# A transformer of top-1 and top-4 expert layers: the landing waits inside GpSimd's runs of indirect transfers, taken out of the top-4 layers

## The reference, cut to what matters

```python
x = x + 0.5 * top1(norm(x))       # 8 experts, hidden 512, one expert per token
x = x + attention_a(norm(x))      # 8 heads of 128
x = x + 0.5 * top1(norm(x))
x = x + 0.5 * top4(norm(x))       # 32 experts, hidden 128, four per token, and a shared expert of 512
x = x + attention_b(norm(x))      # 16 heads of 8, rotated
x = x + 0.5 * top4(norm(x))

def top4(x):
    scores = softmax(x @ router_w.T + bias)
    w, idx = top_k(scores, 4); w = w / clip(w.sum(), 1e-12)
    h = silu(x @ gate[e].T) * (x @ up[e].T)            # for each of the token's four experts e
    out = sum over the four of w[e] * (h @ down[e].T)
    return out + (silu(x @ sgate.T) * (x @ sup.T)) @ sdown.T
```

## Time and profile before

| | |
|---|---|
| median of 3 runs | 1868.67 us (1867.82 to 1871.08) |
| the profiled execution's own time | 1873.8 us |
| its span, first to last instruction | 1872.0 us |
| PE busy | 1221.8 us (65%) |
| DVE busy | 1135.0 us (61%) |
| POOL busy | 968.9 us (52%) |
| ACT busy | 785.3 us (42%) |
| first top-4 layer, first scatter to the next layer's start | 640.6 to about 1034 us of the span |
| second top-4 layer, first scatter to the end | 1473.5 to 1872 us |

### The profile page before, as it was taken

One profiled execution on the slowest core, in us unless ns is written; L12 is line 12 of the kernel. 1 busy time (PEld: TensorE's weight loads), 2 busy tenths in 40 slices (PEclk: granted clock), 3 DMA queues, 4 the chain that ended last, 5 costly groups with the idle time before them and its releaser, 6 DMA issues.

```text
span 1872.0 us, 34469 instructions
## 1 busy us (share of the span) xinstructions
PE 1221.8 (65%) x11513; PEld 902.4 (48%) x11545; DVE 1135.0 (61%) x2883; ACT 785.3 (42%) x1164; POOL 968.9 (52%) x1052
## 2 busy tenths in 40 slices
PE   2298577874594165979654578777874085979661
PEld 2297455653494024968522244444433035969420
DVE  6546756767357951424467699898987942325442
ACT  2153356661252022534311388887883022535210
POOL 0624234551623276636675377666651376646664
PEclk9998789995796577989967555555555587989886
DMA  9233134410231013645311000000000014536312
GB/s 348 65 96 95 36 123 149 147 54 2 93 90 43 13 49 109 197 132 185 124 48 42 13 2 2 2 1 2 1 2 1 23 48 139 188 131 192 96 49 78
DMA packets 100000, 150.44 MB, mean 80 GB/s; under 512 B 21409, under 2 KB 54817, under 8 KB 99105
## 3 DMA queue, kind: packets, MB, share of 16 engines
q1 hardware_dynamic: 58656, 75.30, 12.3%
q0 software_dynamic: 20480, 41.98, 7.5%
q10 hardware_dynamic: 20736, 31.47, 5.2%
HBM read 74.16 MB, written 74.45 MB: 79 GB/s over the span
## 4 chain that ended last, share of the span: by engine, by line
PE 33%; POOL 19%; DVE 18%; issue 14%; DMA 8%; SPq 4%; ACT 2%; DVEq 0%; ACTq 0%; another core or an unknown queue 0%; POOLq 0%
POOL slots_top L624 14%; POOL AREA L1086 5%; PE PS L845 4%; PE PS L906 4%; DMA slots_top<-XN,ROW 3%; PE PS L298 3%; SPq L1285 3%; DVE X L1107 3%; PE PS L300 3%; PE PS L299 3%; PE PS L1729 2%; PE PS L928 2%; DVE AREA L1895 2%; PE PS L1745 2%; PE PS L1717 2%
## 5 line engine op out<-in xcount | busy, mean ns | idle before, releaser
L624 POOL DMA_INDIRECT slots_top<-XN,ROW x320 | 317.3, 992 | 322.8 <-DVE ROW L578 183.6
L1086 POOL DMA_INDIRECT AREA<-results_top,ROW x320 | 305.2, 954 | 275.2 <-DMA results_top<-AREA 125.1
L998 DVE SCALAR_TENSOR_TENSOR AREA<-PS,AREA 128x512 f32<-128x512 f32 x96 | 66.4, 691 | 254.2 <-ACT AREA L975 251.6
L1690 POOL TENSOR_TENSOR AREA<-AREA 128x1024 f16<-128x1024 f32 x64 | 151.4, 2365 | 91.5 <-ACT AREA L1830 91.3
L906 PE MATMUL PS<-WGU,AREA 128*128 x768 | 187.0, 388 | 0.0
L1919 DVE TENSOR_REDUCE AREA<-PS 128x4 f32<-128x1024 f32 x128 | 156.1, 1219 | 30.4 <-PE PS L1717 29.6
L1823 ACT ACTIVATE AREA<-PS,AREA 128x1024 f32<-128x1024 f32 x128 | 142.6, 1114 | 53.1 <-PE PS L1729 52.9
L906 PEld LDWEIGHTS PS<-WGU,AREA 128*128 128x128 f32 x768 | 142.3, 195 | 16.5 <-ACT AREA L965 0.2
L1318 POOL TENSOR_TENSOR AREA<-AREA 128x1536 f16<-128x1536 f32 x32 | 92.9, 2902 | 102.7 <-ACT AREA L1533 102.7
L417 PE MATMUL PS<-IDF,XN 128*128 128x128 f32 x192 | 49.7, 417 | 134.6 <-DVE XN L407 134.6
L1830 ACT ACTIVATE AREA<-AREA 128x1024 f16<-128x1024 f32 x128 | 135.5, 1059 | 0.0
(11 more groups left out here) (260 smaller groups left out, 3584.9 us busy)
## 6 DMA issues: line engine op xcount, KB each, us to landing
AREA<-slots_top SPq DMA_DIRECT2D x96, 256.0 KB
results_top<-AREA ACTq DMA_DIRECT2D x96, 256.0 KB
slots_top<-ZERO SPq DMA_DIRECT2D x24, 512.0 KB, 3.1
AREA<-slots_top SPq DMA_DIRECT2D x48, 128.0 KB
results_top<-AREA ACTq DMA_DIRECT2D x48, 128.0 KB
AREA<-query_rows SPq DMA_DIRECT2D x48, 128.0 KB, 2.8
slots_top<-XN,ROW POOLq DMA_INDIRECT x320, 2.2
AREA<-results_top,ROW POOLq DMA_INDIRECT x320
```

Source lines behind the costliest of these rows:

```text
L624: nc.gpsimd.indirect_dma_start(out=L.xs[q], out_offset=bass.IndirectOffsetOnAxis(ap=ROW[:, n:n + 1], axis=0), in_=XN[:, t * D:(t + 1) * D] ...
L1086: nc.gpsimd.indirect_dma_start(out=slots[L.tag][u][:, c * D:(c + 1) * D], out_offset=None, in_=L.ys[g * GT // L.tiles], in_offset=bass.Ind ...
L1690: nc.gpsimd.tensor_tensor(PB1[1][:, g, :], PF1[:, g, :], PB1[0][:, g, :], ALU.subtract).then_inc(b_plo[1].sem, 1)
```

## The change

Two conditions are changed. In the top-4 layers GpSimd no longer waits for a landing within dispatch (12 waits a layer, the last of each part among them) nor within combine (12 waits a layer). The top-1 layers keep every wait that they had. The waits for row numbers, for stored results and for a buffer that was added stay everywhere, and so do the waits of SP and DVE for the landings that they need.

```diff
@@ dispatch_pool
                     in_=XN[:, t * D:(t + 1) * D], in_offset=None).then_inc(dp_sent[q].sem, 16)
-                every = (16, 8)[q] if L is L1 else (0, 4)[q]
+                every = (0, 4)[q] if L is L0 else 0
                 if every and n % every == every - 1:
                     pool.wait_ge(*dp_sent[q].at(16 * (n % (L.tiles * L.K) + 1)))
@@ combine_pool
                     ).then_inc(cb_got[u].sem, 16)
-                    if c % 8 == 7 and (g < NG // 2 or c < GK - 1) or L is L0 and c == 3 and g < NG // 2:
+                    if L is L0 and c == 3 and g < NG // 2:
                         pool.wait_ge(*cb_got[u].at(16 * (L.turn[g] * GK + c + 1)))
```

## The result

The changed kernel takes **1806.78 us** (median of 4 runs, 1800.57 to 1807.19) where the one before takes 1868.66 us (1867.82 to 1871.08) on the same chip: a ratio of 0.9664, 95% interval 0.965 to 0.9677, so 3.4% faster. Forecast were 1805 us. The profiled execution took 1806.83 us, with a span of 1805.0 us against 1872.0 us before.

The account below looks back on a forecast made before the run. GpSimd's dispatch and combine in the two top-4 layers were taken to bound the kernel. 26.6 + 37.5 = 64.1 us, less 0.6 us, gave 1810.3 us profiled and a predicted median of 1805 us, range 1798 to 1833 us.

Parts of the forecast that it names:

- The removed waits cost their idle time: Full gain in both top-4 layers: 26.6 and 37.5 us from subtracted idle times; chance 0.76.
- Part 1, the dispatch: Top-4 dispatch: without its waits, part 1's blocks come 17.5 us and 19.8 us earlier in the two layers.
- PE's readiness: Before part 1's blocks: PE ready 15.6 and 16.8 us earlier, data 16.0 and 17.2 us; the smaller counts.
- The slow start between the parts: PE's first slow matmuls after its pause before part 1 go with the pause: 1.9 and 3.0 us.
- A fall of the clock inside the blocks: Sign of being wrong: PE's granted clock falls in 170 us of pauseless blocks; each 1% at 1.2 GHz costs 1.7 us.
- Part 2: First top-4 layer's combine: DVE's 9.06 us before g3 go as well, so g3's addition is 26.6 us earlier.
- GpSimd's wait for buffers: First top-4 combine: waits for buffers hardly bind; g2 and g3 would start at 862.8 and 882.8 us.
- Part 3: Second top-4 layer's combine: g4 starts 31.3 us earlier, four later waits give 6.2 us; g7's addition 37.5 us earlier.
- The idle time of about 5 us: Second top-4 layer: GpSimd stands about 5 us before g4, put down to DVE's L1107.
- Half of it comes: Rival: back-to-back transfers land late, so dispatch's or combine's gain fails; 1831 or 1842 us, chance 0.11.
- The waits only change their name: Rival: GpSimd's descriptor writing stops anyway, the pause returns inside transfer rows; no gain, 1869 us, chance 0.05.
- slower by GpSimd's descriptor writing: Rival: descriptor writing gets dearer from a run's 17th transfer on, 65 us a layer, about 1998 us; chance 0.08.

Follow-up runs that it names:

- e9: The kernel before, unchanged, run again for its trace: 1869.67 us, ratio 1.0002.
- e11: Against the changed kernel, the landing waits of the top-1 layers removed too: 1805.64 us, ratio 0.9664 to the kernel before.
- e3: Against the changed kernel, the combine's waits of g4 to g7 in the top-4 layers kept: 1813.0 us, ratio 0.9727 to the kernel before.
- e7: Against the changed kernel, top-4 combine groups take buffers in another turn, so g4 waits for no addition: 2279.39 us on the second job's chip.
- e1: Against the kernel before, only the dispatch's waits in the top-4 layers removed: 1831.6 us, ratio 0.982.
- e2: Against the kernel before, only the combine's waits in the top-4 layers removed: 1837.28 us, ratio 0.9862.
- e12: Against the changed kernel, a landing wait after every fourth scatter of the top-4 dispatch: 1902.0 us, ratio 1.0169 to the kernel before.
- control: The changed kernel itself, run on the second job's chip: 2278.34 us, ratio 1.0465 to the kernel before.

## Why the prediction was right, and where it was not

**The removed waits cost their idle time.** Right: 26.6 and 37.5 us forecast, 25.6 and 36.6 us measured; the sum 64.1 against 62.2 us, the median 1805 against 1806.78 us. That single terms fit to 1 us is in part luck: `e9`'s trace in the place of before's would give 28.5 and 33.2 us. The sum, then 61.8 us, isn't luck.

**Part 1, the dispatch.** 17.5 and 19.8 us forecast at the first gather, 16.6 us (199.62 to 183.02 us from the first scatter) and 19.6 us (201.87 to 182.27 us) measured. The data are there 15.95 and 17.1 us earlier, by the last scatter's start (16.0 and 17.2 forecast), and PE's readiness is the smaller count, as forecast: no pause is left between the parts, and 3.9 instead of 3.7 us came off before part 0. The slow start between the parts did go. What is missing in the first layer, 0.9 us, is less than what two executions of the kernel before differ by: in `e9` the first gathers come at 201.3 and 199.3 us. In this execution part 0's first L906 took 3.64 us, against 2.92 us before. After g0's addition L906 is slow once more, at 2.72 us, with a granted clock of 0.83 in the 10 us around it. A fall of the clock inside the blocks was one of the signs of being wrong, and it came, if briefly: g1 and g2 are 14.9 us earlier where g0 is 16.6 us earlier, so it took 1.7 us. It doesn't come from the change, though. PE stands there for 1.9 us in `e9` as well, which has the slow step too (24.7 us from g0's addition to g1's, as in after), and `e11`, without the waits, has none (23.1 us, as in before). PE in order of time, and the window (the last three columns are clock, DMA share and GB/s):

```profile
858.17 1.21 PE L928 MATMUL PS<-WD,AREA 128*128 x8 [1.88 <-DVE AREA L993]
...
860.88 2.72 PE L906 MATMUL PS<-WGU,AREA 128*128 x8
```

```profile
856.00:866.00 10.00, 8.12 (x46) 7.30 (x45) 4.81 (x10) 3.02 (x6) 7.56 (x9) 0.83 0.52 147
```

**Part 2.** Right: the 9.06 us before g3 are gone, g3 comes 24.1 us earlier (26.6 forecast, the difference being these 0.9 and 1.7 us of part 1), and g7 25.8 us. That the waits of g4 to g7 are free here is shown by `e3`. GpSimd's wait for buffers was called hardly binding; it stood 2.07 us before g3, which g3's gathers had to spare.

**Part 3.** Right in both terms: g4's start is followed by g7's addition after 81.7 us, 87.8 us before, so 6.1 us against 6.2. g4 itself starts 30.5 us earlier behind the first scatter, where 31.3 us were forecast. The idle time of about 5 us before it is 3.98 us and put down to L1107. That name is less than it seems: by `e7`, on the other chip, the stored results hold g4 just as long, as the prediction had them come "at about the time of g2's addition". `e3`, whose kept waits should cost these 6.1 us and 0.8 us in the first layer, stands 12 us above the whole by its ratio and 6 us by its median; its trace is the closer witness: 89.4 us from g4's start to g7's addition against 81.7, so 7.7 us, and one of its four waits was a dear one, 3.5 us.

**The rivals.** "Half of it comes" fell with the result, and `e1` and `e2` show that both halves came. "The waits only change their name" and "slower by GpSimd's descriptor writing" fell with rows of 0.96 us and 1.26 us apart through 128 scatters, on both chips. The Trainium skill's 2.0 us for a transfer ("DMA: Bandwidth & Descriptors", Anatomy of one DMA) would have given 2 us more; the trace stays with its own 1.24 us in the quiet, though `e12`'s mean of 1.47 us shows what traffic adds. The limit of which the Trainium skill speaks ("Debugging Trainium Hangs", Descriptor Overflow) wasn't met at 128 transfers in a run.

**What the working left out.** "Slower" came, 4.65%, on the chip of the second job, by neither of the mechanisms weighed. Every price was taken from a trace of one chip, and nothing in that trace hints at another one where a pause on GpSimd keeps ACT and DVE going. The forecast holds for chips like the one measured, and that the result came from such a chip is luck as far as the prediction goes.

## What to carry to other kernels

A landing wait of GpSimd cost its idle time less the issue time that stays, and that passed to the end only where the next engine was already idle for it. Count it layer by layer, as here 62 us in the top-4 layers and nothing in the top-1 layers with waits of the same kind. Where pauses between long runs of GpSimd's indirect transfers look idle, measure on more than one chip before they go: the same kernel gained 3.4% on one and lost 4.65% on another, so the choice between the two versions isn't settled by the median of one.

## What the hardware showed unexpectedly

- One of the four jobs' chips takes 2184 us for a kernel that the others run in 1865 to 1870 us, with GpSimd's rows, the loads' landing times (19.9 us for PJ's 2 MB on both) and the numbers of instructions unchanged. The control's excess over the first chip, 465 us of span, lies 33 us before the first top-4 layer, 234 us from there to the second, and 198 us in the second. A slower PE is only a small part of it: PE is busy for 1268.0 against 1217.3 us.
- On it, only what PE signals is seen to come late in the stall looked at; what ACT signals to DVE and PE is prompt.
- ACT's starts after a stall there come at distances of 16.79, 28.00, 16.80, 39.20 and 8.40 us, close to multiples of 2.8 us. No run explains it.
- 128 indirect transfers in one run, one every 1.26 us, don't slow GpSimd's own rows and bring no wait on GpSimd, on either kind of chip.
